# Sixteen neighbouring pixels a partition, in one run, in the loads for the first statistics

## The reference, cut to what matters

```python
def _L0_conv_ref(x):            # WINDOW = (1, 5, 20), FILL = 1.0
    w0, w1, w2 = WINDOW
    s = box_sum(box_sum(x, 1, w0), 2, w1)
    num = box_sum(s * s, 3, w2)
    d = box_sum(box_sum(box_sum(x * x, 1, w0), 2, w1), 3, w2)
    c0 = box_sum(jnp.ones((x.shape[1],), x.dtype), 0, w0)
    c1 = box_sum(jnp.ones((x.shape[2],), x.dtype), 0, w1)
    norm = c0[:, None] * c1[None, :]
    denum = d * norm[None, :, :, None]
    return jnp.nan_to_num(num / denum, nan=FILL)

def _gn(v, G=32, eps=1e-5):
    B_, H_, W_, C_ = v.shape
    g = v.reshape(B_, H_, W_, G, C_ // G)
    m = jnp.mean(g, axis=(1, 2, 4), keepdims=True)
    s = jnp.var(g, axis=(1, 2, 4), keepdims=True)
    return ((g - m) / jnp.sqrt(s + eps)).reshape(v.shape)

x = x + _L0_conv_ref(_gn(x))
x = x + _L1_conv_ref(_gn(x))
```

## Time and profile before

| | us |
|---|---|
| median of 3 runs | 5891.36 (5890.29 to 5891.37) |
| the profiled execution | 5891.84 |
| its span in the trace | 5890.1 |
| busy: PE, PEld, DVE, ACT, POOL | 5516.2, 5490.1, 4830.7, 4491.4, 4585.6 |
| start of pair 1, of pair 15, and of the copy of totals at L683 | 20.64, 267.35, 305.42 |

### The profile page before, as it was taken

How to read it: one execution, slowest core, us unless ns; L and a number is a source line. 1 busy time by engine, 2 the same in 40 slices (tenths; PEclk the granted TensorE clock), 3 DMA queues, 4 the chain that set the end, 5 groups by cost and what they waited for, 6 DMA issues and landing times.

```text
span 5890.1 us, 145274 instructions
## 1 busy us (share of the span) xinstructions
PE 5516.2 (94%) x53804; PEld 5490.1 (93%) x53804; DVE 4830.7 (82%) x8140; ACT 4491.4 (76%) x6153; POOL 4585.6 (78%) x1427
## 2 busy tenths in 40 slices
PE   0089999999999999999999999999999999999999
PEld 0089999999999999999999999999999999999999
DVE  7888889988889999999999777777777777777776
ACT  0068777777777788878887788888888888888887
POOL 0056665566658899989998899999999999999998
PEclk9999999999999999999999999999999999999999
DMA  9966565565643343433434344443434343434343
GB/s 358 347 214 214 197 228 196 193 214 207 221 150 129 129 171 128 169 130 139 160 136 164 129 146 153 143 156 140 159 137 162 135 165 131 168 129 170 128 171 128
DMA packets 664736, 1007.81 MB, mean 171 GB/s; under 512 B 5168, under 2 KB 664624, under 8 KB 664624
## 3 DMA queue, kind: packets, MB, share of 16 engines
q1 hardware_dynamic: 664624, 1006.65, 48.7%
HBM read 603.98 MB, written 402.65 MB: 171 GB/s over the span
## 4 chain that ended last, share of the span: by engine, by line
PE 67%; DVE 4%; ACT 0%; issue 0%; POOLq 0%; POOL 0%; DVEq 0%; ACTq 0%
PE width_ps L526 34%; PE num_ps L554 18%; PE den_ps L563 14%; DVE recip L741 1%; DVE y_both L752 1%; DVE lane_mv L636 1%; DVE den_ps L734 1%; DVE out_stats L629 1%; PE den_ps L554 0%; DVE mid L727 0%; ACT recip L448 0%; DVE stat_two L683 0%; DVE beside_stats L629 0%; ACT top L429 0%; ACT recip L441 0%
## 5 line engine op out<-in xcount | busy, mean ns | idle before, releaser
L343 POOL TENSOR_TENSOR centred<-x_both,mean_row 128x1536 f32<-128x1536 f32 x512 | 1773.6, 3464 | 997.4 <-PE width_ps L526 690.1
L554 PE MATMUL num_ps<-band_c,sT 128*128 128x138 f32 (+2 forms) x12288 | 1812.0, 284 | 30.0 <-DVE y_both L752 29.2
L352 POOL TENSOR_TENSOR y_both<-x_both,y_both 128x1536 f32<-128x1536 f32 x512 | 1775.7, 3468 | 17.5 <-DVE y_both L752 17.5
L526 PE MATMUL width_ps<-band_wc,square 128*128 128x130 f32 x12288 | 1652.0, 277 | 17.0 <-DVE mid L727 12.5
L554 PEld LDWEIGHTS num_ps<-band_c,sT 128*128 128x128 f32 x12288 | 1609.4, 190 | 38.8 <-DVE y_both L752 14.2
L526 PE MATMUL width_ps<-band_w,centred 128*128 128x130 f32 x12288 | 1562.6, 276 | 0.0
L526 PEld LDWEIGHTS width_ps<-band_wc,square 128*128 128x128 f32 x12288 | 1507.4, 191 | 19.9 <-DVE mid L727 10.1
L526 PEld LDWEIGHTS width_ps<-band_w,centred 128*128 128x128 f32 x12288 | 1459.9, 191 | 0.4
L441 ACT ACTIVATE recip<-den_ps,bias_ln 128x768 f32<-128x768 f32 x1024 | 920.2, 899 | 644.1 <-PE den_ps L563 449.3
L734 DVE SCALAR_TENSOR_TENSOR den_ps<-den_ps,recip 128x768 f32<-128x768 f32 x1024 | 987.4, 964 | 498.1 <-ACT recip L448 471.6
L360 POOL TENSOR_TENSOR low<-mid 128x1536 bf16<-128x1536 f32 x384 | 1055.2, 2748 | 283.2 <-DVE mid L727 283.2
(11 more groups left out here) (55 smaller groups left out, 2877.2 us busy)
## 6 DMA issues: line engine op xcount, KB each, us to landing
x_both<-in_x_dram SPq DMA_DIRECT2D x80, 3072.0 KB, 11.0
first_layer_out<-y_both SPq DMA_DIRECT2D x64, 3072.0 KB, 18.3
x_both<-first_layer_out SPq DMA_DIRECT2D x64, 3072.0 KB, 10.9
out_dram<-y_both SPq DMA_DIRECT2D x63, 3072.0 KB, 18.2
beside<-in_x_dram SPq DMA_DIRECT2D x30, 3072.0 KB, 10.9
y_both<-in_x_dram SPq DMA_DIRECT2D x18, 3072.0 KB, 18.7
out_dram<-y_both SPq DMA_DIRECT2D x4, 768.0 KB, 3.5
```

The source lines that it names most:

```text
L343: nc.gpsimd.tensor_tensor(centred[e % 2][:], x_in[slot][:, g * PSEG:(g + 1) * PSEG, :], mean_row[ph % 2][:].unsqueeze(1).to_broadcast([P, ...
L352: nc.gpsimd.tensor_tensor(y_out[slot][:, g * PSEG:(g + 1) * PSEG, :], x_in[slot][:, g * PSEG:(g + 1) * PSEG, :], y_out[slot][:, g * PSEG:( ...
L526: last = nc.tensor.matmul(bank[:, at:at + WN], data[:, r * 2 + j, P * k:P * (k + 1)], band[:, j, :], start=(r == 0 and j == 0), stop=(r == ...
L554: last = nc.tensor.matmul(bank[:, lo:hi], data[:, k, at:at + P], band_c[k][:], start=(k == 0), stop=(k == KB - 1), skip_group_check=True)
```

## The change

The four loads of each turn of `measure_loads` take another view of the same image. With it, partition p of a tile holds the sixteen pixels 16p to 16p + 15, which lie together in DRAM, and the destination is written as one run of 16 x 384 numbers a partition. A tile covers the same 2,048 pixels as before. The other loads, and everything on the other engines, are as before; line numbers after L215 go up by one.

```diff
@@ -213,6 +213,7 @@
             def _(sp):
 
                 view = tiles_of(x, 0)
+                runs = x[0].rearrange("h w c -> (h w) c").rearrange("(t p s) c -> p t s c", p=P, s=SEGS)
 
                 def measure_loads(i, lo):
                     for s in range(4):
@@ -221,7 +222,7 @@
                             sp.wait_ge(tile_measured, i * 2 + s // 2 - 1)
                         if lo == TILES // 4 - 1 and s >= 2:
                             continue
-                        sp.dma_start(stat_tiles[s][:], view[:, bass.ds((i * 4 + s) * SEGS, SEGS), :]
+                        sp.dma_start(stat_tiles[s][:].unsqueeze(1), runs[:, bass.ds(i * 4 + s, 1), :, :]
                                      ).then_inc(in_landed[s], 16)
                 looped(sp, TILES // 4, measure_loads, [0, TILES // 4 - 1])
```

## The result

| | before | after |
|---|---|---|
| median, us | 5890.94 (20 runs) | 5878.35 (20 runs) |
| profiled execution, us | 5891.84 | 5877.14 |
| its span | 5890.1 | 5875.4 |
| start of pair 15 | 267.35 | 252.77 |
| start of the copy of totals | 305.42 | 290.85 |

The changed kernel is 12.6 us faster; the ratio is 0.998 with a 95% interval of 0.9973 to 0.9986, which is 8 to 16 us. I had forecast 17.8 us. The time of 5878.35 lies in the range, but the gain is 5 us smaller than forecast, and the forecast gain lies just outside of the interval. One run of the kernel before took 16,160 us and is left out here; the others lay between 5889.0 and 5892.7, those of the changed kernel between 5874.3 and 5883.5: it scatters more than twice as much. The profiled execution is among the better ones, with 14.7 us less.

A forecast was written before the change was run, and what follows sets the result against it. The opening was taken as paced by each buffer's cycle of measuring, issue, latency and moving; faster moving brings pair 15 17.8 us sooner, so 5891.4 - 17.8 = 5873.6 us, range 5866 to 5883.

The forecast's parts named there:

- The bound: Opening: DVE waits 49.9 us for DMA; loads are on the path, and time won there comes off the end.
- The rate: Opening loads: 912 ns a packet of 24,576 B, 431 GB/s; moving a pair (D) takes 14.59 us, not 16.83.
- the ceiling at 374 GB/s: Rival, opening loads: reading is capped at 374 GB/s, so nothing changes and the time is 5891 us; chance 0.07.
- the cut pieces: Rival, opening loads: the chip cuts runs into pieces, 15.34 us a pair at 4,096 B, 12.0 us gained, 5879.4; chance 0.09.
- the slower loads: Rival, opening loads: partitions 24 KiB apart meet on the same memory parts; 19.24 us a pair, 5918 us; chance 0.06.
- What stays: Measuring a pair stays 14.81 us, pair 15 to the copy 38.1 us; pair 16's loads and the reload stay covered.
- The round: One buffer's opening cycle: measuring 14.81, issue 0.18, latency 2.69, moving 14.59; 32.27 us for two pairs, was 34.5.
- L: Latency in a buffer's opening cycle, beyond measuring, the 0.18 us until issue and moving: 2.69 us, held fixed.
- the first rival: Opening loads: fewer runs also cut the latency from 2.69 to 2.0 us, 4.8 us more gained, 5868.8; chance 0.12.
- Pair 8: Opening: it has landed while pair 7 is measured and starts at 130.0 us, not 141.39; 11.4 us gained.
- The walk: Pair-by-pair sum of opening starts: gains of 2.24 us at pair 1, 8.9 at pair 7, 17.8 at pair 15.
- theory A: From the experiments, opening loads: the loss comes from idle-queue restarts and unequal engine finishes, both growing with packet length.

The follow-up runs named there:

- far: The changed kernel with the partitions of one load 768 KiB apart in DRAM, not 24 KiB: 5879.54 us, 11.1 us gained against the kernel before.
- run2: The changed kernel with opening runs of 3,072 B (two neighbouring pixels) in place of 24,576 B: 5881.25 us, 9.4 us gained against the kernel before.
- run4: The changed kernel with opening runs of 6,144 B (four neighbouring pixels) in place of 24,576 B: 5877.85 us, 12.8 us gained against the kernel before.
- run8: The changed kernel with opening runs of 12,288 B (eight neighbouring pixels) in place of 24,576 B: 5879.60 us, 11.0 us gained against the kernel before.
- three16: The changed kernel's 24,576 B runs plus a third buffer (pair of tiles) in the opening: 5857.99 us, ratio 0.9945 to the kernel before.
- three1: The kernel before, its 1,536 B runs kept, plus a third buffer (pair of tiles) in the opening: 5886.30 us, ratio 0.9993.
- three4: The kernel before with a third buffer (pair of tiles) in the opening and runs of 6,144 B: 5862.62 us, ratio 0.9952.

## Why the prediction was right, and where its size was off

**The bound: right.** The waits for DMA shrank by 14.5 us and the profiled execution by 14.7; nothing else moved.

**The rate: right.** A line through two packet sizes of the trace before gave 912 ns a packet and 431 GB/s; the trace has 913 and 433. This drops three rivals at once: the ceiling at 374 GB/s, the cut pieces (415 or less), and the slower loads, whose supposed cause (distance in DRAM) left the packets of far as they were. The prediction says that nothing in the trace before is longer than 2 KB; the page before has 112 packets of 8 KB and more, all code loads, so long packets had been seen, if only few. Its reading of the Trainium skill's page "DMA: Bandwidth & Descriptors", section "Latency and other measured facts", as no loss at 512 KiB is a little too good, as the page has 207 GB/s there against 214 in full; that 24 KiB gives no loss was the prediction's own extension, and 913 ns a packet bears it out. The sentence on the limit of 358 GB/s (the Trainium skill's page "DMA: Bandwidth & Descriptors", section "Where 436 GB/s comes from") was right to go by the trace: 374 GB/s before, 433 after.

**What stays: right, with less room than forecast.** The pair's 14.81 us and the 38.1 us from pair 15 to the copy are as forecast. The halves of pair 16 were issued only 1.2 us before pair 15 (251.54 to 252.77), and not 2.3 to 2.5. So the reload ended 3.1 us before its first user (290.4 for POOL's 293.55), where it had been 4.3 us (303.8 for 308.12; the prediction read 5). Nothing waited for it.

**The round: mis-sized.** The step that failed is "With D = 14.59 the round is 14.81 + 0.18 + 2.69 + 14.59 = 32.27 us". It took L from the kernel before and held it fixed. From pair 1 to pair 7 the round is (116.69 - 18.53) / 3 = 32.72 us, so L is 3.14. That is the opposite of the first rival, by which fewer runs would shorten it. Issuing did get shorter (two loads take 0.88 us of SP where they took about 3), but the very first packet starts at 1.92 us in the kernel before and at 1.84 in the changed one, 1.1 and 1.0 us after the first issue.

The packets and the ends of the loads divide L in three. The means are over the six odd pairs that DVE waits for after pair 1 (3, 5, 7, 11, 13, 15), in one trace of each kernel, in us:

| | before | run2 | run4 | run8 | changed | far |
|---|---|---|---|---|---|---|
| issue to the mean end of the 16 DMA engines, less the moving | 1.74 | 1.81 | 1.92 | 1.94 | 1.87 | 1.94 |
| mean end to the last engine's end | 0.19 | 0.22 | 0.24 | 0.75 | 0.59 | 0.87 |
| last engine's end to DVE's start | 0.71 | 0.67 | 0.66 | 0.63 | 0.57 | 0.54 |
| L | 2.65 | 2.71 | 2.82 | 3.31 | 3.03 | 3.35 |

So the slow start costs only 0.1 to 0.2 us more with long packets: the first packet is slow by 0.66 us, but in the kernel before the start was slow too. What grew is the lateness of the last DMA engine, from 0.2 to 0.6 to 0.9 us, and it did so between 6,144 and 12,288 B. A round up to pair 7 is 0.45 us longer than forecast: over pairs 3, 5 and 7 the last engine's lateness grew by 0.49 us (0.21 to 0.70), the start by 0.13, and the stretch up to DVE's start shrank by 0.15.

**Pair 8: wrong.** "Pair 8 has landed while pair 7 is measured": it hadn't. The walk let an even pair's loads follow the odd pair's without a gap. Pair 4's loads were issued at 48.28, 2.5 us before the last DMA engine had finished pair 3, and yet the mean end of its engines came 15.84 us after that of pair 3, not 14.59. With pair 12, issued 2.1 us ahead, it is 15.80; with pair 2, issued 16 us ahead, 14.60. So with these packets a lead of 2 us doesn't hide the start, and 1.2 us are lost. run4 lost only 0.13 us at its pair 12, with a lead of 2.3 us; why it did and run8 (1.16) didn't isn't shown. The even pairs, which had next to nothing to spare in my walk, are late by that, and then by the same late engines: from pair 4 on DVE waits 1.0 to 1.7 us before each even pair but pair 10. By the pairs of the walk, the shortfall is 0.1 us at pair 1, 0.7 at pair 3, 1.5 at pair 7, 2.7 at pair 8 and 3.3 at pair 15.

So theory A is borne out as a whole: in the two traces of 24,576 B the packets in full flow are as fast as forecast, what is lost is lost around the restarts, and nothing is missing in three16, whose queue never runs dry. Of its two halves the late DMA engines are the larger. Why they finish further apart with packets of 12,288 B and more was not found, and far's and run8's single traces lost more there (6.9 and 5.9 us) than the changed kernel's (3.2). Nor do I know why the median run is 1.2 us slower than the profiled one; its trace was not taken.

## What to carry to other kernels

A DMA-bound stage with two buffers that are reloaded only once they are read has a round of read + issue + latency + move, shared by two; a faster move gives half of what it saves, and a third buffer turns the sum into a maximum. Two packet sizes in one trace give the rate of a third by a straight line, but not what a restart costs. Here the last of the 16 DMA engines finished later behind the others with packets of 12,288 B and more, and once the overhead per packet was a few per cent (4% at 6,144 B) longer runs gained nothing that could be measured as long as the queue ran dry between loads. Where a load is waited for, look at its last DMA engine and not at the mean rate, and look for the code loads. When one fix gives less than its sum, try it together with the one that keeps the queue full: 12.6 and 4.3 us made 32.6.

## What the runs showed of the hardware that I had not expected

- After an idle queue, the first packet of 24,576 B takes 1.58 us on each DMA engine and the following ones 0.91; but with 1,536 B the first packets take 0.48 us in place of 0.07, so a slow start isn't a matter of long packets. From the issue to the mean end of the engines a restart cost 1.74 us over the moving with 1,536 B and 1.87 with 24,576 B.
- At the end of a load the last of the 16 DMA engines comes 0.2 us after their mean with packets of up to 6,144 B, and 0.6 to 0.9 us after it with 12,288 and 24,576 B.
- Loads of 24,576 B packets that are issued 2.1 to 2.5 us before the load ahead has ended lose 1.2 us (pairs 4 and 12); issued 16 us before, nothing (pair 2).
- Each code load of 8,192 B in a queue that was never empty set one DMA engine back by 0.8 to 1.0 us for good, with data packets of 1,536, 6,144 and 24,576 B alike (three1, three4, three16).
- Runs of 6,144 B reach 416 GB/s, and 24,576 B reach 433, from one core that reads alone.
- Partitions 24 KiB or 768 KiB apart in DRAM gave the same 913 and 914 ns a packet.
